# Macaron layer on one core: the experts' gate and up products change sides of the matmul, and GpSimd's sums of the expert stages go to VectorE

## The reference, cut to what matters

```
x = x + 0.5 * ffn(layernorm(x))
x = x + attention(layernorm(x))
x = x + 0.5 * ffn(layernorm(x))

ffn:  logits = flat @ router_w.T;  top 4 of 64 experts per token, softmax weights of the four
      xg = flat[tok_table]                                   # 64 experts x 32 places x 256
      g, u = einsum('ecd,efd->ecf', xg, gate_w), einsum('ecd,efd->ecf', xg, up_w)      # f = 64
      y = einsum('ecf,edf->ecd', silu(g) * u, down_w)
      out = zeros.at[tok_table].add(y * w_table)
      out = out + shared experts (512 wide): (silu(flat @ sg.T) * (flat @ su.T)) @ sd.T
```

## Time and profile before

| | before |
|---|---|
| median of 3 runs | 967.13 us (966.71 to 968.01) |
| the profiled execution, its own time | 967.17 us |
| its span, first to last instruction | 965.4 us |
| PE busy | 926.2 us (96%) |
| DVE busy | 762.4 us (79%) |
| ACT busy | 647.0 us (67%) |
| POOL busy | 645.3 us (67%) |
| mean granted TensorE clock | 0.995 of full speed |

### The profile page before, as it was taken

One profiled execution on the slowest core, in us unless ns is written; L12 is line 12 of the kernel. 1 busy time (PEld: TensorE's weight loads), 2 busy tenths in 40 slices (PEclk: granted clock), 3 DMA queues, 4 the chain that ended last, 5 costly groups with the idle time before them and its releaser, 6 DMA issues.

```text
span 965.4 us, 18681 instructions
## 1 busy us (share of the span) xinstructions
PE 926.2 (96%) x5851; PEld 560.8 (58%) x5859; DVE 762.4 (79%) x2083; ACT 647.0 (67%) x1426; POOL 645.3 (67%) x613
## 2 busy tenths in 40 slices
PE   7999889999999999999999999999999999988987
PEld 4766556555555555555555555555555555765666
DVE  7854399988888888888888888888878789875247
ACT  6534446887877787787778778777777777643431
POOL 3367779987576768778676766867677465326642
PEclk9999999999999999999999999999999999999999
DMA  8889745667666879798895766767675565385757
GB/s 344 350 267 310 274 155 164 109 132 121 137 142 105 164 147 191 154 204 175 169 188 98 158 109 130 153 99 144 107 155 90 97 112 96 71 330 175 255 209 272
DMA packets 302979, 165.60 MB, mean 172 GB/s; under 512 B 278176, under 2 KB 285600, under 8 KB 300832
## 3 DMA queue, kind: packets, MB, share of 16 engines
q1 hardware_dynamic: 297696, 146.56, 65.0%
q0 software_dynamic: 3072, 9.44, 2.9%
q10 hardware_dynamic: 2112, 8.39, 2.2%
HBM read 68.93 MB, written 28.31 MB: 101 GB/s over the span
## 4 chain that ended last, share of the span: by engine, by line
PE 76%; DVE 11%; DMA 4%; issue 3%; POOL 3%; ACT 2%; SPq 1%; DVEq 0%; POOLq 0%; ACTq 0%
PE b_o L110 5%; PE b_p L110 5%; PE b_o L111 5%; PE b_o L112 5%; PE b_p L112 5%; PE b_p L111 5%; PE b_s L111 5%; PE b_s L112 5%; PE b_s L110 5%; PE b_out L110 3%; PE b_out L112 3%; PE b_out L111 3%; PE b_v L110 2%; PE b_v L112 2%; PE b_v L111 2%
## 5 line engine op out<-in xcount | busy, mean ns | idle before, releaser
L2499 POOL TENSOR_TENSOR h<-pr,h 128x512 f16<-128x512 f32 x256 | 293.1, 1158 | 157.7 <-ACT h L1205 152.3
L1195 ACT ACTIVATE pr<-b_s,nmax,kappa 128x512 f32<-128x512 f32 x256 | 197.6, 774 | 38.3 <-DVE nmax L1953 35.2
L1950 DVE TENSOR_SCALAR_CACHE_REDUCE junk<-b_s 128x512 bf16<-128x512 f32 x256 | 174.9, 683 | 22.6 <-PE b_s L112 17.5
L1205 ACT ACTIVATE h<-pr 128x512 f16<-128x512 f32 x256 | 153.4, 626 | 3.5 <-DMA pT<-h 3.1
L1981 DVE SCALAR_TENSOR_TENSOR x<-b_out,rinv,x 128x256 f32<-128x256 f32 x256 | 111.3, 475 | 42.2 <-PE b_out L112 40.5
L110 PE MATMUL b_p<-xh,w 128*128 128x512 f16 x256 | 97.8, 382 | 2.8 <-DVE xh L1738 2.4
L110 PE MATMUL b_o<-pT,v 128*128 128x512 f16 x256 | 97.0, 379 | 1.7 <-DVE oT L1969 1.7
L112 PE MATMUL b_p<-xh,w 128*128 128x512 f16 x256 | 97.7, 382 | 0.0
L111 PE MATMUL b_p<-xh,w 128*128 128x512 f16 x256 | 97.6, 381 | 0.0
L110 PE MATMUL b_s<-kT,qT 128*128 128x512 f16 x256 | 97.0, 379 | 0.0
L111 PE MATMUL b_s<-kT,qT 128*128 128x512 f16 x256 | 97.0, 379 | 0.0
(11 more groups left out here) (230 smaller groups left out, 2240.9 us busy)
## 6 DMA issues: line engine op xcount, KB each, us to landing
raw<-in_experts SPq DMA_DIRECT2D x32, 768.0 KB, 7.7
raw_cs<-in_heads SPq DMA_DIRECT2D x16, 1024.0 KB, 5.0
zrows<-zero ACTq DMA_DIRECT2D x4, 2048.0 KB, 12.4
z<-zrows SPq DMA_DIRECT2D x16, 512.0 KB, 4.1
zrows<-zero SPq DMA_DIRECT2D x16, 512.0 KB, 4.2
zl<-zrows SPq DMA_DIRECT2D x16, 512.0 KB, 9.8
rows<-xn SPq DMA_DIRECT2D x8, 512.0 KB, 10.7
pT<-h SPq DMA_TRANSPOSE x256, 3.3
```

Of the source, the lines that this page charges most:

```text
L1195: act.activation(pr[n % 4][:], b_s[n % 3][:], ACT.Exp, bias=nmax[:, u % 2, i:i + 1], scale=kappa[:, s:s + 1], accum_out=rsum[:, u % 2, i:i ...
L1205: act.activation(h[n % 4][:, 0, :], pr[n % 4][:], ACT.Copy).then_inc(q["p_high"], 1)
L1950: dve.tensor_scalar(junk[n % 2][:], b_s[n % 3][:], 0.0, None, ALU.add, ALU.max, accum_out=peaks[:, n % 2:n % 2 + 1]).then_inc(q["peak_read ...
L2499: pool.tensor_tensor(h[n % 4][:, 1, :], pr[n % 4][:], h[n % 4][:, 0, :], ALU.subtract).then_inc(q["p_split"], 1)
```

## The change

- `expert_in`: the experts' gate and up weights are now the weights of the array (128 x 64 each), the tokens stream (32 columns). A group takes 16 matmuls in place of 8. The result has f on the partitions: experts 0 and 2 on partitions 0 to 63, experts 1 and 3 on 64 to 127.
- `expert_hidden` on PE and on ACT (the turn of `ehid` and the copy of it) are gone. DVE's `expert_hidden` writes [128 x 64] straight to `ehT`, which has four buffers now.
- `b_act` has two banks (`rl0` and `up1`, where `b_h` was), so `expert_in(G)` waits for the multiplication of group G-2 and not of G-1.
- The orders of PE and ACT in both expert stages are new: in the steady state PE runs `expert_in(G)`, `expert_out(G-1)`, `turn_expert(G+2)`.
- `hidden_low` of 6, 7, 8, 22, 23, 24 and 25 and, for the first pair of heads, the two `range_weights`, `high_weights` and `low_weights` of the queries and keys are moved from POOL to DVE.

```diff
-        ehid = [m.at(Dm + 19968 + 512 * s, f"ehid{s}", [P, 2, F]) for s in range(2)]
-        ehT = [m.at(Dm + 20992 + 512 * s, f"ehT{s}", [P, P]) for s in range(2)]
+        ehT = [m.at(Dm + 19968 + 256 * s, f"ehT{s}", [P, F]) for s in range(4)]
...
-        b_x, b_h, b_act, b_y = gate1[:, 0:D], up1[:, 0:P], rl0[:, 0:P], rl1[:, 0:D]
+        b_x, b_act, b_y = gate1[:, 0:D], (rl0[:, 0:P], up1[:, 0:P]), rl1[:, 0:D]
...
-                if G > 0:
-                    pe.wait_ge(q["ehid_done"], G)
-                if G == QK_AT:
+                if G > 1:
+                    pe.wait_ge(q["ehid_done"], G - 1)
+                if G >= QK_AT and G % 2 == 0:
                     pe.wait_ge(q["qk_ready"], 1)
-                for k in range(DC):
-                    for e in range(EG):
-                        ins = pe.matmul(b_act[e * CAP:(e + 1) * CAP, :], xgT[s][:, k, e * CAP:(e + 1) * CAP],
-                                        gate_up_of(G, k, e), start=(k == 0), stop=(k == DC - 1))
+                for wt in range(2):
+                    for pair in range(EG // 2):
+                        for k in range(DC):
+                            for half in range(2):
+                                e = 2 * pair + half
+                                ins = pe.matmul(b_act[s][half * F:(half + 1) * F, F * wt + CAP * pair:F * wt + CAP * (pair + 1)],
+                                                gate_up_of(G, k, e)[:, wt, :], xgT[s][:, k, e * CAP:(e + 1) * CAP],
+                                                start=(k == 0), stop=(k == DC - 1))
                 ins.then_inc(q["act_done"], 1)
 
-            def expert_hidden(G):
+            def expert_out(G):
                 pe.wait_ge(q["ehid_done"], G + 1)
-                pe.wait_ge(q["sb_h"], G)
-                pe.transpose(b_h, ehid[G % 2][:].rearrange("p h f -> p (h f)"), ident[:]).then_inc(q["h_turned"], 1)
...
-                    ins = pe.matmul(b_y[e * CAP:(e + 1) * CAP, :], ehT[s][e % 2 * F:(e % 2 + 1) * F, e * CAP:(e + 1) * CAP],
+                    ins = pe.matmul(b_y[e * CAP:(e + 1) * CAP, :], ehT[G % 4][e % 2 * F:(e % 2 + 1) * F, e // 2 * CAP:(e // 2 + 1) * CAP],
                                     down_of(G, e), start=True, stop=True)
...
(DVE)
+            def hidden_low(n):
+                dve.wait_ge(q["hhi_done"], n + 1)
+                dve.wait_ge(q["hlo_done"], n)
...
+                dve.tensor_tensor(hT[1][:, n % SM, :], hid[n % 2][:], f32(hT[0][:, n % SM, :]), ALU.subtract
+                                  ).then_inc(q["hlo_done"], 1)
...
-                dve.tensor_tensor(ehid[s][:], b_act[:, F:2 * F].unsqueeze(1).broadcast_to([P, 2, F]),
-                                  esil[s][:].unsqueeze(1).broadcast_to([P, 2, F]), ALU.mult).then_inc(q["ehid_done"], 1)
+                if G >= 4:
+                    dve.wait_ge(q["y_done"], G - 3)
+                dve.tensor_tensor(ehT[G % 4][:], b_act[s][:, F:2 * F], esil[s][:], ALU.mult).then_inc(q["ehid_done"], 1)
```

More of the change, by code:

```diff
@@ L397, in gate_up @@
                     pe.wait_ge(q["sb_x"], NG * (lap + 1))
[L398 removed]
+                    pe.wait_ge(q["ehid_done"], NG * (lap + 1))
                 if n >= 2:
@@ L1147, in expert_silu @@
                     act.wait_ge(q["ehid_done"], G - 1)
[L1148 to L1154, removed]
+                act.activation(esil[G % 2][:], b_act[G % 2][:, 0:F], ACT.Silu).then_inc(q["esil_done"], 1)
             def expert_out(G):
@@ L1285, in _ @@
             expert_silu(1)
-            expert_hidden(0)
-            expert_silu(2)
-            gathered(3)
-            silu(8)
-            gathered(4)
             expert_out(0)
             hidden_high(7)
+            gathered(3)
+            expert_silu(2)
+            silu(8)
+            expert_out(1)
+            gathered(4)
             expert_silu(3)
+            expert_out(2)
             gathered(5)
-            expert_hidden(1)
             squares_qk(0)
+            expert_silu(4)
@@ L1297, in _ @@
+            expert_out(3)
             gathered(6)
-            expert_silu(4)
-            expert_hidden(2)
-            expert_out(1)
-            expert_hidden(3)
+            silu(9)
             expert_silu(5)
-            expert_out(2)
-            expert_hidden(4)
+            expert_out(4)
             gathered(7)
             expert_silu(6)
-            expert_out(3)
+            expert_out(5)
+            gathered(8)
             expert_silu(7)
-            gathered(8)
-            expert_out(4)
@@ L1311, in _ @@
-            expert_hidden(5)
+            expert_out(6)
             gathered(9)
             expert_silu(8)
-            expert_hidden(6)
-            expert_out(5)
-            expert_hidden(7)
-            expert_hidden(8)
+            expert_out(7)
             gathered(10)
-            expert_out(6)
             expert_silu(9)
+            expert_out(8)
             gathered(11)
             expert_silu(10)
-            expert_out(7)
+            expert_out(9)
+            gathered(12)
             expert_silu(11)
-            gathered(12)
@@ L1326, in _ @@
-            expert_hidden(9)
-            silu(9)
-            expert_out(8)
+            expert_out(10)
+            gathered(13)
             expert_silu(12)
-            gathered(13)
-            expert_out(9)
-            expert_hidden(10)
-            expert_silu(13)
+            expert_out(11)
             gathered(14)
             hidden_high(8)
-            expert_hidden(11)
+            expert_silu(13)
+            expert_out(12)
             gathered(15)
             hidden_high(9)
-            expert_out(10)
@@ L1340, in _ @@
-            expert_hidden(12)
-            expert_out(11)
+            silu(10)
             expert_silu(14)
-            silu(10)
-            expert_hidden(13)
-            expert_out(12)
             expert_out(13)
             expert_silu(15)
-            expert_hidden(14)
+            hidden_high(10)
             expert_out(14)
-            expert_hidden(15)
-            hidden_high(10)
             expert_out(15)
@@ L1657, in _ @@
             hidden_high(25)
-            gathered(27)
-            expert_hidden(26)
+            expert_out(25)
             gathered(28)
             expert_silu(27)
-            silu(26)
-            expert_out(25)
+            expert_out(26)
             gathered(29)
             expert_silu(28)
-            expert_hidden(27)
-            expert_out(26)
-            expert_hidden(28)
+            expert_out(27)
             gathered(30)
             expert_silu(29)
-            expert_out(27)
             expert_out(28)
-            expert_hidden(29)
+            gathered(31)
+            silu(27)
             expert_silu(30)
             hidden_high(26)
-            gathered(31)
-            expert_hidden(30)
             expert_out(29)
@@ L1680, in _ @@
             expert_out(30)
-            expert_hidden(31)
-            silu(27)
             expert_out(31)
@@ L2039, in _ @@
             expert_hidden(3)
+            hidden_low(6)
             hidden(8)
@@ L2046, in _ @@
             add_shared(0)
+            hidden_low(7)
             expert_hidden(5)
@@ L2065, in _ @@
             expert_hidden(13)
+            hidden_low(8)
+            low_weights(0)
             expert_hidden(14)
+            low_weights(1)
             expert_hidden(15)
@@ L2329, in _ @@
             slot_weights(17)
+            hidden_low(22)
             slot_weights(18)
+            hidden_low(23)
             expert_hidden(17)
@@ L2354, in _ @@
             expert_hidden(26)
+            hidden_low(24)
             expert_hidden(27)
+            hidden_low(25)
             expert_hidden(28)
@@ L2591, in _ @@
             gather(8)
-            hidden_low(6)
             gather(9)
@@ L2598, in _ @@
             scatter(2)
-            hidden_low(7)
             gather(12)
@@ L2778, in _ @@
             gather(23)
-            hidden_low(22)
-            hidden_low(23)
             gather(24)
@@ L2794, in _ @@
             scatter(21)
-            hidden_low(24)
             scatter(22)
@@ L2798, in _ @@
             scatter(24)
-            hidden_low(25)
             scatter(25)
```

165 lines of the change are left out of this document (67 added, 98 removed).

## The result

The changed kernel takes **983.47 us** (median of 4 runs, 983.03 to 984.22), the kernel before took 967.57 beside it (966.71 to 968.23). The ratio is **1.0156, 95% interval 1.0143 to 1.0169**: slower by 15.9 us. Forecast were 971.1 and a range up to 976, so the direction was right and the size was not. The page of the profile gives a mean granted clock of 0.988 where before has 0.995, and that is where to look first.

What follows compares the result with a forecast made beforehand. PE was taken to bound both expert stages; lap 0 +0.1, lap 1 +3.4 and tail +0.4 made +3.9 on 967.17, so 971.1 us, with an 8-in-10 range of 962.5 to 976.

Steps and rivals of the forecast that it cites:

- the sum itself: Whole kernel: lap 0, lap 1 and tail together +3.9 on 967.17, giving 971.1 us.
- The new `expert_in`, 1.04 us: PE's gate and up block per group: 1.04 us in place of 0.57, with both array halves loading side by side.
- The halves do load side by side: Assumed in expert_in; the rival without it had 1.97 us a block, 1,000 us in total, chance 0.04.
- A group at 1.98 us: PE's cost of one steady-state group: 0.37 + 1.04 + 0.57 = 1.98 us in place of 1.62.
- Lap 0, +0.1: Lap 0's expert groups: expert_in +7.5, turns -2.6, waits -4.8, together +0.1 us.
- The old waits: PE's waits in the expert groups, to go with the second bank and new order: 4.8 and 1.5 us won.
- Attention, 0: The attention stretch between the two expert stages: unchanged.
- Lap 1, +3.4: Lap 1's expert groups: expert_in +7.1, turns -2.2, waits -1.5, together +3.4 us.
- The tail, +0.4: Behind the last expert_out: PE stands still 0.8 us longer before gate_up(28), half of it covered, +0.4 us.
- The sums moved to DVE, 0: Seven hidden_low and six weight steps, about 9 us of DVE work, fit in its free time: costed at nothing.
- No load during a stream: Rival in expert_in: loads and streams take turns, 1.53 us a block, +15, 986 us in total; chance 0.05.
- 60% busy: Expected sign in the changed profile: ACT below 60% busy in both laps' expert stages.

Runs made afterwards that it cites:

- h1: Kernel after with gate_up(25) moved to right behind expert_in(16), and ACT's expert_out(14) ahead of hidden_high(10): 970.8 us, 1.0029 of the kernel before.
- g1: Kernel after with gate_up(25), 12 matmuls of 512 columns, moved from behind turn_expert(25) to right behind expert_in(16): 973.7 us, 1.0057 of the kernel before.
- f3: Kernel before with only the seven hidden_low and six weight steps moved to DVE, on a slower chip: 997.1 us, 0.9993 of the kernel before.
- e4: Kernel after with the seven hidden_low and six weight steps back on POOL, on a slower chip: 1000.8 us, 1.0049 of the kernel before.
- f1: Kernel after with 16 filler matmuls after expert_out(16) and 16 after expert_out(27), on a slower chip: 1007.6 us, 1.0094 of the kernel before.

## Why the prediction was wrong, by its own steps

**The step that failed is the sum itself: every block was taken at the clock that the kernel before had there**, and no term or rival asked whether the new form would keep it. In lap 1 it did not: the clock was at half for 20.5 us, and that cost 8.7. Without it the rest nearly stands: h1, where lap 1's groups have the full clock, took 970.8 us. That this is 0.3 from the forecast is in part luck, since h1's two changes of order also won time that the forecast did not have (lap 0 ends 0.6 us earlier than before, forecast 0.1 later).

- *The new `expert_in`, 1.04 us*: right, 1.05. The halves do load side by side: the load is 138 ns in the median (132 to 138), as in the earlier trace rows, and 32 of them take 1.01 us, so one starts every (1.01 - 0.138) / 31 = 0.028 us on average, where in `candidates`, all in one half, it was every 0.058.

```profile
926.69 1.01 PEld L490 LDWEIGHTS rl<-xgT,raw 128*64 128x64 f32 x32 [0.36 <-issue]
```

  That is PEld's timeline of the kernel after. With no overlap at all the loads alone would take 32 x 0.138 = 4.4 us. The rule of the Trainium skill (TensorE: Matmul & The Clock Gate, Part 3, "The mechanism"), by which a load overlaps a matmul in flight only over different rows of the array, was priced at 1.53 us a block; the trace is against it, as the earlier trace rows were. That rival's price was also too low for what it said: a load of 0.138 and a stream of 0.027 in strict turn, 16 times, would be 2.6 us.
- *A group at 1.98 us*: right at full clock (1.98). At half it is 3.48, and this is the term that the sum had wrong.
- *Lap 0, +0.1*: measured +0.6 (the last `expert_out` ends at 109.50 against 108.90 before). The old waits went as forecast; ACT's new order brought the one of 2.5 us. The prediction checked which engine could keep up on average, not what stands ahead of which step on it. h1 has -0.6.
- *Attention, 0*: measured +1.7 (lap 1's first turn is 2.3 later than before, 884.43 against 882.16, of which 0.6 is lap 0's). The kernel before has its one short fall (3.4 us) at 140.1 us, the kernel after at 158.6. From the end of lap 0's last `expert_out` to that turn it is 773.3 us before and in h1, which has no fall there at all, and 774.9 in the kernel after and in g1, with falls at 110.0 and 133.9. That the place of these short falls is the cause is argued from these times, not shown.
- *Lap 1, +3.4*: measured +13.8. From the second `expert_in` to the start of `down(5)` it is 905.75 - 888.80 = 16.95 us in the kernel after and 900.27 - 890.50 = 9.77 in g1 for the same blocks, and from there to the next `expert_in` 7.39 against 5.83: 7.18 + 1.56 = 8.7 us are the clock. The other 5.1 are my terms, under-sized by 1.7. The waits of lap 1 won next to nothing: 1.00, 0.56, 0.52, 0.69 and 0.25 (3.0 us) stand where 1.34, 0.52, 0.49, 0.46, 0.24 and 0.21 (3.3) stood, and I had counted 1.5 won.
- *The tail, +0.4*: measured +0.3 (981.8 - 942.54 = 39.26 from the last `expert_out`'s end to the end of the span, against 965.4 - 926.46 = 38.94). PE's `gate_up(28)` waits 0.96 us for DVE.
- *The sums moved to DVE, 0*: right by f3, alone. In the new orders (e4) it is open.
- *Rivals*: none had the cause. "No load during a stream" gave 986 us, near the measured number, by a block of 1.53 that does not exist. A rival can come near the time by accident, so it is the row and not the total that decides.

Sum: 0.6 + 1.7 + 13.8 + 0.3 = 16.4 us, as the spans differ (981.8 - 965.4).

## What to carry to other kernels

Price a block twice, at both levels of the clock, whenever a change thins out what TensorE does, and look for the waits in front of it: here the waits cost 2 us, and the fall behind them 8.7. If a thin stretch must follow waits, try a dense piece of real work in them, not behind them; here that was worth 9.9 us in the kernel after, and nothing in the kernel before, whose clock had held. And when an engine's order is rewritten, read what stands ahead of each step on it, since "60% busy" hides a wait of 2.5 us for another engine.

## What was not expected of the hardware

- A TensorE that is busy without a gap can stay at 1.2 GHz: in the kernel after PE is busy in 18.36 of 18.36 us from 890.94 at a granted clock of 0.50. Its falls in lap 1's groups last 17 to 24 us (kernel after, A and B), with 32 small instructions (64 weight columns, 32 streamed) between the others in each group, and end 0.9 to 4.1 us after the next dense piece starts. 16 fillers (f1) ended them in the same way. With the old product falls in lap 1's groups lasted 3.4 to 6.8 us, but one of the kernel before in lap 0 on B 13.7.
- The same instructions at half clock don't take twice as long: `expert_in` 1.85 against 1.05 (1.76 times), `expert_out` 1.01 against 0.57.
- On the chips called B the kernel before takes 996 to 999 us in place of 968. In its trace ACT, PE and POOL halt for 1.5 to 2.2 us while the first groups' rows are gathered in lap 0, and the clock falls to half behind that, at 68.2 us. This is the timeline of the kernel before on B; "remote" and "issue" mean that no work of this core in the profile ends the wait:

```profile
67.13 0.22 ACT L1148 ACTIVATE esil<-rl 128x64 f32<-128x64 f32 x1 [2.06 <-remote]
67.83 0.77 PE L488 MATMUL rl<-raw,xgT 128*32 128x128 f32 x16 [2.20 <-issue]
68.79 0.94 POOL L2428 DMA_INDIRECT xg<-rows,tok_i  x1 [1.50 <-remote]
```

  What stops them is not known. It is a reason to compare totals within one chip only.
